# Attention scores in two rows of pairs for each group instead of four, query blocks regrouped (3 and 0, 2 and 1), and the value products in two halves inside the rows

## What is computed

```python
qkv = x @ w_qkv                      # 32 query heads, 8 key/value heads, 16 wide
xq = _apply_rope(xq); xk = _apply_rope(xk)
keys = jnp.repeat(xk, N_REP, axis=1) # N_REP = 4 query heads share one key head
scores = jnp.einsum('bhsd,bhtd->bhst', xq, keys) * scale
scores = jnp.where(causal, scores, -jnp.inf)
probs = jax.nn.softmax(scores, axis=-1)
out = jnp.einsum('bhst,bhtd->bhsd', probs, values)
...
a = _anemll_linear(x, gate_w, gate_su, gate_sv)   # w_eff = w * (su @ sv)
b = _anemll_linear(x, up_w, up_su, up_sv)
d = jax.nn.silu(a) * b                            # 1792 hidden columns
...
x = x + _L0_attn_ref(xn, ...) + _L0_ffn_ref(xn, ...)
```

## Time and profile before

| | us |
|---|---|
| median of 3 runs | 663.43 |
| lowest and highest | 663.38, 663.96 |
| the profiled execution | 663.49 |
| its span (first to last instruction) | 661.8 |
| PE busy in the span | 652.9 (99%) |
| DVE busy | 415.8 (63%) |
| ACT busy | 287.5 (43%) |
| POOL busy | 241.1 (36%) |

### The profile page before, as it was taken

One profiled execution on the slowest core, in us unless ns is written; L12 is line 12 of the kernel. 1 busy time (PEld: TensorE's weight loads), 2 busy tenths in 40 slices (PEclk: granted clock), 3 DMA queues, 4 the chain that ended last, 5 costly groups with the idle time before them and its releaser, 6 DMA issues.

```text
span 661.8 us, 9993 instructions
## 1 busy us (share of the span) xinstructions
PE 652.9 (99%) x3486; PEld 497.2 (75%) x3486; DVE 415.8 (63%) x987; ACT 287.5 (43%) x558; POOL 241.1 (36%) x242
## 2 busy tenths in 40 slices
PE   7999999999999999999999999999999999999998
PEld 7786666666666666666787878888888888888886
DVE  6967877767767777672477665377565555646501
ACT  4334455455455455444344334254434444343321
POOL 3596233123323233322144638503234332323443
PEclk9999999999999999999999999999999999999999
DMA  9548423252323222021254510500001110112011
GB/s 296 137 136 169 133 80 111 78 133 88 95 58 90 79 79 78 18 81 49 76 188 160 191 35 4 159 1 33 32 33 33 63 33 33 32 33 80 11 55 63
DMA packets 23401, 55.17 MB, mean 83 GB/s; under 512 B 3860, under 2 KB 4344, under 8 KB 22296
## 3 DMA queue, kind: packets, MB, share of 16 engines
q1 hardware_dynamic: 22840, 54.41, 27.8%
q10 hardware_dynamic: 512, 0.13, 0.1%
HBM read 42.86 MB, written 11.54 MB: 82 GB/s over the span
## 4 chain that ended last, share of the span: by engine, by line
PE 92%; DMA 2%; POOL 2%; DVE 1%; SPq 1%; issue 1%; ACT 1%; DVEq 0%; ACTq 0%
PE bank L52 25%; PE bank L53 24%; PE bank L54 24%; PE bank L1089 7%; PE bank L1120 6%; PE bank L1107 2%; PE bank L180 2%; DMA wqkv_raw<-in_w_qkv 1%; PE bank L1096 1%; PE bank L344 1%; PE bank L108 1%; POOL wqkv_lo L531 1%; DMA k_stack<-k_hi 1%; PE bank L1676 1%; DMA q_lo<-rope_lo 1%
## 5 line engine op out<-in xcount | busy, mean ns | idle before, releaser
L1036 DVE CUSTOM_DVE_ANT_0 bank<-bank,mask 128x512 f32<-128x512 f32 (+3 forms) x256 | 118.3, 522 | 44.0 <-PE bank L1089 43.9
L217 POOL TENSOR_TENSOR up_w_lo<-up_w_eff,up_w_hi 128x512 fp32r<-128x512 f32 x50 | 66.9, 1344 | 106.4 <-ACT up_w_hi L213 106.4
L382 POOL TENSOR_TENSOR down_h_lo<-hidden,down_h_hi 128x512 fp32r<-128x512 f32 x50 | 66.2, 1325 | 88.3 <-ACT down_h_hi L377 88.3
L988 ACT ACTIVATE probs<-bank 128x512 f32<-128x512 f32 x160 | 84.7, 596 | 25.3 <-PE bank L1107 25.3
L52 PE MATMUL bank<-x0T_hi,up_w_hi 128*128 128x512 f32 x224 | 95.0, 424 | 0.0
L54 PE MATMUL bank<-x0T_lo,up_w_hi 128*128 128x512 f32 x224 | 88.6, 395 | 0.0
L53 PE MATMUL bank<-x0T_hi,up_w_lo 128*128 128x512 f32 x224 | 88.4, 395 | 0.0
L52 PE MATMUL bank<-down_w_hi,down_h_hi 128*128 128x512 f32 x200 | 78.5, 392 | 0.4 <-DVE bind_cols L1396 0.4
L53 PE MATMUL bank<-down_w_hi,down_h_lo 128*128 128x512 f32 x200 | 78.0, 390 | 0.0
L945 POOL TENSOR_SCALAR_AFFINE_SELECT probs<-probs 128x512 f32<-128x512 f32 x64 | 39.9, 635 | 100.6 <-ACT probs L988 100.6
L377 ACT ACTIVATE down_h_hi<-hidden 128x512 fp32r<-128x512 f32 x50 | 31.6, 631 | 91.8 <-PE bank L54 91.8
(11 more groups left out here) (167 smaller groups left out, 1391.1 us busy)
## 6 DMA issues: line engine op xcount, KB each, us to landing
w_raw<-in_w_gate_up SPq DMA_DIRECT2D x25, 512.0 KB, 3.4
w_raw<-in_w_down SPq DMA_DIRECT2D x25, 256.0 KB, 3.0
q_stack<-q_hi SPq DMA_DIRECT2D x32, 128.0 KB, 3.4
att<-att_T SPq DMA_DIRECT2D x16, 256.0 KB, 2.1
q_hi<-rope_hi SPq DMA_DIRECT2D x8, 256.0 KB
q_lo<-rope_lo SPq DMA_DIRECT2D x8, 256.0 KB
q_stack<-q_lo SPq DMA_DIRECT2D x16, 128.0 KB, 3.3
attention_or_xn<-att SPq DMA_DIRECT2D x16, 128.0 KB
```

The lines of the kernel that those rows point to most:

```text
L217: pool.tensor_tensor(self.half(self.w_lo[:, o % 2], k), self.half(self.w_eff, k), f32(self.half(self.w_hi[:, o % 2], k)), ALU.subtract).th ...
L382: pool.tensor_tensor(self.h_lo[:, k % 2, :], self.hid[:, o, b * S:(b + 1) * S], f32(self.h_hi[:, k % 2, :]), ALU.subtract).then_inc(self.h ...
L988: act.activation(pt[:, BLOCK_OF[KEY_PIECES[p]], :, :], narrow.bank(("keys", g, p))[:, :].rearrange("p (h s) -> p h s", h=REP), ACT.Exp).th ...
L1036: dve.tensor_tensor_reduce(out=own, in0=own, in1=e.mask[:, S - w:S], scale=1.0, scalar=NEG, op0=ALU.add, op1=ALU.max, accum_out=rmax[:, i ...
```

## The change

- Two bursts for each group instead of four. A burst comes after every sixth step (`LEAD, EVERY = 1, 6`: after steps 6, 12, ... 204, and 210 with values alone). `FACTOR_EVERY = 3` keeps the weight factors at the steps at which they were.
- `PARTS = [(3, 0), (2, 1)]`: the query blocks 3 and 0 are one part (`OUTER`), 2 and 1 the other (`INNER`). The outer burst has 5 pieces of maxima (four heads of block 3 with 512 keys, and one piece with the four heads of block 0) and 5 of keys; the inner burst has 6 of maxima (four of block 2 with 384 keys, two of block 1 with two heads by 256 keys each) and 5 of keys.
- The values come in two halves, `values(g, part)`: the outer half of group n-1 in the inner burst of n, the inner half of n-2 in the outer burst of n. They stand between the second and the third pair of the burst (`PAIRS_BEFORE_VALUES = 2`). The outer half has for key block 0 one product over the two query blocks 0 and 3 and for the others one over block 3 (16 matmuls for the four heads), the inner half 12 matmuls. So there are 28 matmuls for each group instead of 16, over the same number of columns.
- ACT copies each half out by itself, between the exponentials.
- The turn of a part stands at the end of the burst after the one that has its maxima, and always in the ring `wide`.

```diff
-LEAD, EVERY = 4, 3
-MAX_BURST = [(0, 2), (2, 5), (5, 8), (8, 11)]
-KEY_BURST = [(0, 2), (2, 5), (5, 8), (8, 10)]
+LEAD, EVERY, FACTOR_EVERY = 1, 6, 3
+PARTS = [(3, 0), (2, 1)]
+MAX_PIECES = [(3, h, 1) for h in range(4)] + [(0, 0, 4)] + [(2, h, 1) for h in range(4)] + [(1, 0, 2), (1, 2, 2)]
+MAX_BURST = [(0, 5), (5, 11)]
+KEY_PIECES = [(j, i) for part in PARTS for i in part for j in range(i + 1)]
+KEY_BURST = [(0, 5), (5, 10)]
+PAIRS_BEFORE_VALUES = 2
...
         def stages_of(t):
-            n, k = divmod(t, 4)
...
+            n, part = divmod(t, 2)
+            at = lambda g: g if 0 <= g < GROUPS else None
+            return dict(part=part, maxima=at(n), keys=at(n - 1), values=at(n - 1 if part == INNER else n - 2),
+                        values_of=1 - part, row=at(n if part == INNER else n - 1), row_of=1 - part)
...
-            def values(g):
-                pe.wait_ge(masked, NJ * (g + 1))
-                narrow.free(pe, ("values", g))
+            def values(g, part):
+                pe.wait_ge(masked, NJ * g + 2 * (part + 1))
+                narrow.free(pe, ("values", g, part))
...
-                    if s["values"] is not None:
-                        values(s["values"])
...
+                    for n in range(max(len(maxima), len(keys))):
+                        if n == PAIRS_BEFORE_VALUES and s["values"] is not None:
+                            values(s["values"], s["values_of"])
+                        if s["maxima"] is not None and n < len(maxima):
+                            max_scores(s["maxima"], maxima[n])
+                        if s["keys"] is not None and n < len(keys):
+                            key_scores(s["keys"], keys[n])
+                    if s["row"] is not None:
+                        minus_max(s["row"], s["row_of"])
```

More of the change, by code:

```diff
@@ L857, in attention_stage, with outer_blocks @@
                 s = stages_of(burst_after(step))
-                if s["values"] is not None:
[L859 to L871, removed]
+                if s["maxima"] is not None:
+                    for p in range(*MAX_BURST[s["part"]]):
+                        wide.place(("maxima", s["maxima"], p), reduced, NJ * REP * s["maxima"] + MAX_END[p])
+                if s["row"] is not None:
+                    wide.place(("minus_max", s["row"], s["row_of"]), neg_copied, 2 * s["row"] + 1 + s["row_of"])
+                keys = list(range(*KEY_BURST[s["part"]])) if s["keys"] is not None else []
+                for p in keys[:PAIRS_BEFORE_VALUES]:
+                    narrow.place(("keys", s["keys"], p), exp_done, KEYS * s["keys"] + p + 1)
+                if s["values"] is not None:
+                    narrow.place(("values", s["values"], s["values_of"]), att_out, 2 * s["values"] + 1 + s["values_of"])
+                for p in keys[PAIRS_BEFORE_VALUES:]:
+                    narrow.place(("keys", s["keys"], p), exp_done, KEYS * s["keys"] + p + 1)
+        def outer_blocks(ap):
+            return ap.rearrange("p (i s) -> p i s", s=P)[:, 0:NJ:NJ - 1, :]
         def load_stack(sp, g):
@@ L990, in exp_piece, with evacuate @@
                                ACT.Exp).then_inc(exp_done, 1)
-            def evacuate(g):
-                act.wait_ge(pv_mm, g + 1)
-                if g >= 2:
+            def evacuate(g, part):
+                act.wait_ge(pv_mm, 2 * g + 1 + part)
+                if g >= 2 and part == OUTER:
                     act.wait_ge(att_stored[g % 2], 16 * (g // 2))
-                act.activation(att[:, g % 2, :], narrow.bank(("values", g))[:, :], ACT.Copy).then_inc(att_out, 1)
+                out, bank = att[:, g % 2, :], narrow.bank(("values", g, part))[:, :]
+                if part == OUTER:
+                    out, bank = outer_blocks(out), outer_blocks(bank)
+                else:
+                    out, bank = out[:, P:3 * P], bank[:, P:3 * P]
+                act.activation(out, bank, ACT.Copy).then_inc(att_out, 1)
             for step in range(STEPS):
@@ L1028, in maxima @@
                 i, h, nh = MAX_PIECES[p]
+                part, slot = PART_OF[i]
                 dve.wait_ge(s1_mm, 11 * g + p + 1)
```

140 lines of the change are left out of this document (67 added, 73 removed).

## The result

| | before | after |
|---|---|---|
| median | 663.6 us | 677.6 us |
| lowest, highest | 663.38, 663.96 | 677.04, 678.5 |
| the profiled execution, its span | 663.49, 661.8 | 677.04, 675.3 |

The change makes the kernel slower: the ratio is 1.0215, with a 95% interval of 1.0203 to 1.0228. Two of the four runs of after held TensorE's full clock (677.04 and 677.17), the other two were granted 0.997 of it in the mean and took 1 us more; terms are compared with the profiled one, +13.55 us.

The account below looks back on a forecast made before the run. PE was taken to bound the kernel, with 92% of the span. The terms -13.6 + 8.0 - 2.1 + 5.5 + 11.1 + 3.6 = +12.5 us on 663.5 gave 676.0 us, range 668.5 to 683.0.

Parts of the forecast that it names:

- Terms 1 to 3: On PE alone: fewer excursions to the pairs -13.6 us, values between pairs +8.0, packing -2.1; together -7.7 us.
- term 2: Values between pairs on PE: extra mode changes and slow first pairs, 0.32 us inside against 0.13 at the head, +8.0 us.
- Term 4: Outer burst: the turn waits for DVE to reduce the third piece, 0.39 us late in 14 bursts, +5.5 us.
- Term 5: Inner burst: sixth piece waits for the third, turn for the fourth; 0.74 us in 15 bursts, +11.1 us.
- Term 6: First three bursts, without values between: DVE's pace sets them, 2.48, 2.78 and 2.74 us, +3.6 us together.
- The gated product: In each fourth burst PE's up product wants it behind DVE's late maxima; given 0, bound 8 x 0.1 = +0.8 us.
- A: Rival: DVE isn't in the way, only changes of mode count, so faster, 655.8 us; chance 0.08.
- B: Rival: PE drains while waiting and starts 0.06 after release, so waits hide changes, 4.1 us less, 671.9 us; chance 0.11.
- C: Rival: keys products also wait for ACT in ring `narrow`, 0.3 us in 31 bursts, 9.3 us more, 685.3 us; chance 0.08.
- D: Rival: waits bite in one kind of burst only, the sum ends within 0.2%, 664 us; chance 0.03.

Follow-up runs that it names:

- short maxima: DVE takes each maximum over only the last 128 keys of its piece: 663.3 us in the changed kernel, 661.8 us in the kernel before.
- values first: Changed kernel with both halves of the values at the head of their burst, ahead of all the pairs: 694.1 us.
- turn first: Changed kernel with the turn of the maxima at the head of its burst instead of its end: 674.4 us.
- third early with either turn: Changed kernel, third piece of maxima alone ahead of the values: 679.8 us with the turn at the burst's head, 672.4 us at its end.
- the two with the gated product first: Changed kernel, gated product ahead of the maxima: alone 679.8 us; with third piece ahead of the values, inner turn right behind them, 674.2 us.
- third early with short maxima: Changed kernel, third piece of maxima alone ahead of the values, turn at the end, each maximum over 128 keys alone: 662.5 us.
- values inside: Kernel before, its 15 sets of values ahead of the first quarter's pairs moved between the first and second pair: 669.2 us.

## Why the prediction was right, point by point

The range held and the time was missed by 1.6 us. By its steps:

- **Terms 1 to 3**, PE's own part, -7.7. Their prices hold: a change from the up products to the pairs costs 0.33 where 0.32 was taken, one from the pairs to the values 0.32: the 0.09 that no row of before showed was right, and the half set takes 1.22 with that of its way out, no fixed cost for a pass among it. Of term 2 the place alone was shown by a run, in the kernel before, with 0.19 for 0.19. Their sum is too large: with short maxima in both kernels and the waits taken off, PE gained about 6.0. Where the 1.7 lie isn't split; one or two hundredths of a microsecond in each of some hundred bursts and changes are enough for them.
- **Term 4**: the turn 1.44 us behind the third piece, as forecast. The short maxima show that it hangs on DVE.
- **Term 5**: the sixth piece 1.16 behind the third and the turn 1.76, as forecast. The third piece ahead of the values takes this wait away (3.18 for 3.64), so it is the latency of that one piece.
- **Term 6**: 2.58, 2.85 and 2.73 for 2.48, 2.78 and 2.74, 0.2 us more.
- **The gated product** was the term that was mis-sized: 0, with a bound of 8 x 0.1, for a measured 8 x 0.12 to 0.20, 1.3 us. It sits where the prediction looked for it, but behind a wait, however short, the next weights aren't loaded ahead, 0.10 us that term 5 had counted at its own wait and this step hadn't.
- **The kernel before's own waits** for DVE were in no term. They are gone in the kernel after, 1.4 us in the stretch (259.2 for 257.8 with short maxima).

So the 14.1 us are about -6.0 of PE's own, +21.5 of waits in the kernel after (20.2 in terms 4 to 6, 1.3 of the gated product) and -1.4 of the waits of before. Against the forecast, 12.5, two misses of 1.7 and 1.3 make it slower and one of 1.4 makes it faster: that the sum came this near is luck, the direction and the size of the waits are not. The half microsecond by which the stretch begins sooner, which brings 14.1 to the 13.55 measured, isn't the change's either as far as is known: over the twelve profiled executions that start lies between 56.8 and 58.5 us.

Of the rivals, A had the sign of PE's part right and was wrong on DVE. Its condition was the third piece reduced within 1.05 us in the outer burst and 0.69 in the inner; it is 1.29 and 1.10, and over 128 keys 0.89 and 0.84. There the outer burst stops waiting and the inner one doesn't, just as the condition says. B falls: the turn starts 0.15 behind its release in the outer burst and 0.14 in the inner one, and with short maxima it comes 0.43 behind a sixth piece that had waited, 0.34 + 0.09, so the reload and the change are both paid. C falls: the keys products wait for ACT 0.7 us in all. D falls with A: both kinds of burst wait, each as long as said.

## What to carry to other kernels

Before small matmuls are bunched to save changes of mode, set the number of banks of their ring times PE's distance of starts (here 3 x 0.23 = 0.69 us) against the latency of the piece that frees a bank (here 1.1 to 1.3 us from product to release): what lies between two bunches is what hides it, and a DVE that is idle a third of the time doesn't shorten it. Something long inside a bunch helps only the pieces ahead of it: with the third piece, the last that the ring holds, ahead of the values too the kernel took 672.4 and not 677.6 us. A ring of more banks wasn't tried. A turn belongs where the mode changes anyway: there it cost 0.02 us, at the head of a bunch 0.11.

## What the runs showed of the hardware that I had not expected

**A dip of the clock.** Six kernels (values first, turn first, third early with either turn, and the two with the gated product first) fell to TensorE's lower level (1.2 GHz) once in their profiled executions, for about 3.5 us, with the third early and the turn last for about 7, soon after the first bursts. Two stretches of the turn first, and then the first of them in the changed kernel:

```profile
64.00:67.50 3.50, 3.05 (x13) 1.88 (x12) 2.90 (x13) 0.27 (x1) 0.00 (x0) 1.00 0.70 262
67.50:71.20 3.70, 3.70 (x12) 2.87 (x11) 2.28 (x9) 0.00 (x0) 0.00 (x0) 0.55 0.00 0
```

```profile
64.00:67.50 3.50, 2.87 (x12) 1.71 (x12) 2.85 (x13) 0.34 (x2) 0.00 (x0) 1.00 0.85 289
```

In the first PE still holds 1.00, and is idle in 0.45 of 3.50 us; in the second it is granted 0.55, and its up products start 0.43 apart instead of 0.23. It costs some 1.5 us. The changed kernel's PE was idle longer in this stretch, 0.63 us, and kept its clock after it. The profiled executions of before, of both kernels with short maxima, of the third early with short maxima and of the values inside kept it too. The executions without a profile show that it isn't a matter of the kernel alone: two of the changed kernel and one of each version of it with short maxima were granted 0.997 in the mean, about what the kernels with one dip had (0.997 and 0.998), and other executions of the same kernels 1.0; of the kernel before none on record was under 0.999. Why some executions dip stays open.

**A short wait costs more than itself**: 0.14 us for 0.03, with the weights not loaded ahead (166.47 above).

**The last keys product** behind four small maxima products comes 0.33 us after the one before it, not 0.23, without any wait, in both kernels that have the third piece early.
